# Attention and expert mix on one core: a prologue in another order, and two expert slots per pass of a shared PSUM bank

## What is computed

```python
xn = _layernorm(x)
# attention, 16 heads of width 8; q = k = v
p = einsum('bsd,ed->bse', xn, Wv) + bv
attn = softmax(einsum('bhqd,bhkd->bhqk', p, p) / sqrt(8))
s = einsum('bsd,ed->bse', einsum('bhqk,bhkd->bhqd', attn, p), Wo) + bo
# 8 experts, the best 2 of each token, weighted
z = layernorm(xn, ln_g, ln_b)
w = top-2 of softmax(z @ rW + rb), divided by their sum
mixed = sum_e w_e * (gelu(z @ W1[e] + b1[e]) @ W2[e] + b2[e])
out = x + s * silu(xn + mixed)
```

## Time and profile before

| | |
|---|---|
| three executions | 628.3, 629.17, 630.58 us; median 629.17 us |
| the profiled execution | 632.46 us, of which the span from the first to the last instruction is 630.7 us |
| PE | 571.2 us busy (91% of the span) |
| ACT | 543.2 us busy (86%), of which 488.9 us in the 512 exponentials |
| DVE, POOL | 240.1 us (38%), 230.1 us (36%) |
| mean granted PE clock | 0.936 |
| step 0 to step 255 by the exponentials | 52.73 to 620.54 us |

### The profile page before, as it was taken

The page is one execution under the profiler, slowest core; times in us unless marked ns, Lnnn a source line. Parts: engine busy times, 40 slices in busy tenths (PEclk is TensorE's granted clock), DMA queues, the critical chain, the costliest instruction groups (busy, mean ns, idle before and its releaser), DMA issues.

```text
span 630.7 us, 11527 instructions
## 1 busy us (share of the span) xinstructions
PE 571.2 (91%) x3990; PEld 232.3 (37%) x3990; DVE 240.1 (38%) x695; ACT 543.2 (86%) x591; POOL 230.1 (36%) x252
## 2 busy tenths in 40 slices
PE   3778884799999999799999999999988999999996
PEld 2553320223344344333444344434334343433221
DVE  5553863573333333113222232223232852223381
ACT  4576663699999999979999999999999999999994
POOL 2364047827777774254211121112203334341000
PEclk9977776799999999869999999999995999999999
DMA  6137697746466655227363445453233654442220
GB/s 164 45 101 219 231 304 276 184 132 149 110 162 133 162 96 116 70 67 160 68 153 99 127 112 132 103 135 108 70 117 108 173 167 139 130 116 83 65 66 19
DMA packets 100989, 81.54 MB, mean 129 GB/s; under 512 B 54219, under 2 KB 92638, under 8 KB 100318
## 3 DMA queue, kind: packets, MB, share of 16 engines
q1 hardware_dynamic: 94270, 71.26, 43.2%
q0 software_dynamic: 6656, 9.48, 4.8%
HBM read 58.07 MB, written 28.39 MB: 137 GB/s over the span
## 4 chain that ended last, share of the span: by engine, by line
PE 74%; ACT 9%; DVE 7%; issue 5%; DMA 4%; SPq 1%; ACTq 0%; DVEq 0%
PE bank_v L1330 35%; PE pair L1276 16%; PE bank_f L1370 8%; PE bank_f L1379 8%; ACT exps L776 7%; DMA p_dram<-w_ring 3%; PE bank_f L1347 2%; PE pair L1236 1%; ACT pre L752 1%; PE bank_f L1343 1%; PE pair L1227 1%; DMA x_tok<-in_L_attn_x 1%; DVE o_turned L1082 1%; PE bank_f L1354 1%; DVE v_tok L863 1%
## 5 line engine op out<-in xcount | busy, mean ns | idle before, releaser
L776 ACT ACTIVATE exps<-pair 128x1024 f32<-128x1024 f32 x512 | 488.9, 1049 | 54.6 <-PE pair L1276 36.3
L1330 PE MATMUL bank_v<-exps,v_tok 128*32 128x512 f32 x2048 | 285.0, 630 | 3.1 <-ACT exps L776 1.6
L687 POOL DMA_INDIRECT o_dram<-o_ring,slot_place x80 | 77.4, 968 | 238.3 <-DVE o_ring L1133 238.0
L1276 PE MATMUL pair<-q_ring,k_ring 26*128 26x512 f32 x1024 | 152.9, 513 | 2.7 <-ACT exps L776 2.1
L1276 PEld LDWEIGHTS pair<-q_ring,k_ring 26*128 26x128 f32 x1024 | 60.7, 188 | 93.4 <-ACT exps L776 54.8
L672 POOL DMA_INDIRECT z_dram<-pre,dest_i x64 | 64.3, 1004 | 52.2 <-DVE place_i L1037 33.3
L1379 PEld LDWEIGHTS bank_f<-w_ring,pre 128*128 128x128 f32 x320 | 46.2, 208 | 72.2 <-issue 43.3
L1124 DVE TENSOR_TENSOR pre<-bank_f,w_ring 128x256 f32<-128x256 f32 x80 | 33.9, 423 | 102.1 <-PE bank_f L1370 102.1
L1379 PE MATMUL bank_f<-w_ring,pre 128*128 128x128 f32 x320 | 62.5, 322 | 9.7 <-ACT pre L752 5.3
L1133 DVE TENSOR_TENSOR o_ring<-bank_f,w_ring 128x128 f32<-128x128 f32 x80 | 23.2, 290 | 124.3 <-PE bank_f L1379 121.1
L679 POOL DMA_INDIRECT place_dram<-token_place,place_i x64 | 61.3, 958 | 19.5 <-issue 19.5
(11 more groups left out here) (154 smaller groups left out, 287.1 us busy)
## 6 DMA issues: line engine op xcount, KB each, us to landing
w_ring<-w_dram SPq DMA_DIRECT2D x80, 192.0 KB
w_ring<-w_dram SPq DMA_DIRECT2D x80, 129.0 KB
q_ring<-p_dram SPq DMA_DIRECT2D x56, 104.0 KB
k_ring<-p_dram SPq DMA_DIRECT2D x56, 96.0 KB
z_dram<-s_tok SPq DMA_DIRECT2D x4, 1280.0 KB, 13.1
z_ring<-z_dram SPq DMA_DIRECT2D x80, 64.0 KB
rows_in_sb<-o_dram SPq DMA_DIRECT2D x16, 256.0 KB, 2.9
p_dram<-z_ring SPq DMA_DIRECT2D x8, 256.0 KB, 2.9
```

The costliest lines, as they stand in the source:

```text
L687: pool.indirect_dma_start(o_dram[:, :], bass.IndirectOffsetOnAxis(slot_place[:, h, 4 * k + i:4 * k + i + 1].bitcast(U32), 0), o_ring[:, q ...
L776: nc.scalar.activation(exps[:, g % ES, 2 * half:2 * half + 2, :], pair[(2 * g + half) % 3][:, :, :], ACT.Exp, scale=SCALE).then_inc(exp_do ...
L1276: ins = nc.tensor.matmul(pair[h % 3][:, j % 2, :], k_ring[32 * j:32 * j + KROWS, n % 2, kt * P:(kt + 1) * P], q_ring[32 * j:32 * j + KROWS ...
L1330: ins = nc.tensor.matmul(bank_v[32 * j:32 * j + 32, :], v_tok[:, (n // HG) * KT + kt, first:first + 32], exps[:, g % ES, j, :], start=(kt ...
```

## The change

**The bank.** One use now holds two slots of a quad (`PAIRS` = 2 uses per quad instead of four): `up` writes all 512 columns of `bank_f` with four matmuls, and DVE reads 128x512 at once; `down` writes 256 columns with four matmuls. So 80 uses stand where 160 stood, and `MOE_STEP` is 2.52. The bursts at the two Gelu stretches (now steps 90 and 185) hold all eight `down` slots of two quads in four uses.

**The early steps.** `count` moves from step 7 to 8, the biases from 4..6 and 8..12 to 9..16, the `norm` uses from 13..18 to 23, 25, ... 33, the ranking of the first half one step later, `zero_z(1)` from step 12 to 8, scaling of the first expert layer from 13..16 to 18..21.

**The prologue.** The second chunk of `x` is loaded earlier; the four warming matmuls at the head of the branch that is taken go; on DVE the third chunk of `norm1` stands ahead of `keep_p(0)` instead of behind it, and `norm2` moves out of the loop over blocks, behind the branch. On SP the high part of blocks 0 and 1 is stored three times, so that units 0 and 1 (eight heads) are each loaded with 8 DMAs, after blocks 3 and 4; `w1_stage`, `rb_bc` and `bo_bc` are loaded behind all blocks; the copy in DRAM covers three batches instead of four and is issued for step 14.

```diff
+EARLY_PARTS = 4
...
-WARM = (4, 4)
+WARM = 4
...
-RANK_AT = ((2, 3, 3, 4, 4, 5), (17, 18, 19, 20, 22, 23))
-COUNT_AT = (7, 24)
-ASSIGN_AT = ((7, 8, 8, 9, 10), (25, 26, 27, 28, 30))
+RANK_AT = ((3, 4, 4, 5, 5, 6), (17, 18, 19, 20, 22, 23))
+COUNT_AT = (8, 24)
+ASSIGN_AT = ((8, 9, 9, 10, 11), (25, 26, 27, 28, 30))
 SCALE_Z_AT = ((5, 6, 7, 8), (18, 20, 22, 23))
-EXP_AT = (10, 21)
+EXP_AT = (11, 21)
 WEIGH_AT = ((12, 13, 14), (31, 32, 33))
-BIAS_AT = 4
+BIAS_AT = 9
+COPY_HI_AT = 14
 BIAS_COLS = 2
-NORM_AT = 12
-ZERO_AT = 12
-SCALE_W1_AT = (13, 14, 15, 16)
-SCATTER_AT = (11, 31)
-MOE_AT = 37
-MOE_STEP = 1.19
+NORM_AT = 23
+ZERO_AT = 8
+SCALE_W1_AT = (18, 19, 20, 21)
+SCATTER_AT = (12, 31)
+MOE_AT = 38
+MOE_STEP = 2.52
 LOAD_LAG = 5
 PLACE_AT = (54, 77)
-BURST = 6
+PAIRS = 2
...
-        for i in range(4):
+
+        for i in range(PAIRS):
             t = max(t, place((kind, q, i), t) + 1 - MOE_STEP) + MOE_STEP
...
-        downs = [("down", first + i // 4, i % 4) for i in range(8)]
-        uses[g] = downs[:BURST]
+        uses[g] = [("down", first + i // PAIRS, i % PAIRS) for i in range(2 * PAIRS)]
         at.update({what: g for what in uses[g]})
-        t = g + 3
-        for what in downs[BURST:]:
-            t = max(t, place(what, t) + 1 - MOE_STEP) + MOE_STEP
-        return g, t
+        return g, g + 3
...
-        place(("norm", g), NORM_AT + g - EARLY)
+        place(("norm", g), NORM_AT + 2 * (g - EARLY))
...
+        def stored(g):
+
+            return 16 * (EARLY_PARTS + g // 2 * PARTS)
...
             load_x(1)
+            load_x(2)
...
+            def load_unit(n):
+                if n >= 2:
+                    sp.wait_ge(pv_done, (n - 1) * US)
+                if n == HG:
+                    sp.wait_ge(hi_copied, 32)
+                    for i in range(2):
+                        sp.wait_ge(m_kept[1 + i], (NB - EARLY) // 2 * 16)
+                tokens = slice((n // HG) * S, (n // HG + 1) * S)
+                for j in range(4):
+                    head = (n % HG) * 4 + j
+                    sp.dma_start(k_ring[32 * j:32 * j + PROWS, n % 2, :].bitcast(F32), p_dram[head, 0:PROWS, tokens]
+                                 ).then_inc(kq_in[n % 2], 16)
+                    sp.dma_start(q_ring[32 * j:32 * j + KROWS, n % 2, :].bitcast(F32), p_dram[head, HI_ROW:HEAD_ROWS, tokens]
...
             for g in range(NB):
                 tokens = slice(g * BLK, (g + 1) * BLK)
                 sp.wait_ge(parts_ready, g + 1)
-                for part in range(PARTS):
-                    row = (HI_ROW, LO_ROW)[part]
-                    sp.dma_start(p_dram[:, row:row + DK, tokens], (p_hi, p_lo)[part][:, g % 2, :]).then_inc(parts_stored[g % 2], 16)
-                if g == EARLY:
+                hi_rows = (0, HI_ROW, LO_ROW + DK) if g < EARLY else (HI_ROW,)
+                for row in hi_rows:
+                    sp.dma_start(p_dram[:, row:row + DK, tokens], p_hi[:, g % 2, :]).then_inc(parts_stored[g % 2], 16)
+                sp.dma_start(p_dram[:, LO_ROW:LO_ROW + DK, tokens], p_lo[:, g % 2, :]).then_inc(parts_stored[g % 2], 16)
+                if g == 2:
                     for e in range(EARLY):
                         sp.wait_ge(n2_copied, e + 1)
                         sp.dma_start(p_dram[:, M_ROW, e * BLK:(e + 1) * BLK], m_blk[:, e, :]).then_inc(m_kept[0], 16)
-                    for i in range(2):
-                        sp.wait_ge(parts_stored[i], 16 * PARTS)
+                elif g == 3:
+                    for e in range(EARLY):
+                        sp.wait_ge(parts_stored[e], stored(e))
                     sp.wait_ge(m_kept[0], 16 * EARLY)
                     sp.wait_ge(m_zeroed, 32)
                     sp.wait_ge(ring_cleared, 1)
-                    for j in range(4):
-                        load_head(0, 0, j, 0, kq_in[0])
-                        load_stabiliser(0, j, kq_in[0])
-                if g == 3:
-                    sp.dma_start(w1_stage, W1.rearrange("e h f -> h e f")).then_inc(w1_staged, 16)
-                    sp.dma_start(rb_bc[:, :], rb.rearrange("(a d) -> a d", a=1).broadcast_to([P, E])).then_inc(bias_in, 16)
-                    sp.dma_start(bo_bc[:, :], bo.rearrange("(a d) -> a d", a=1).broadcast_to([P, D])).then_inc(bias_in, 16)
+                    load_unit(0)
+                elif g == 4:
+                    load_unit(1)
+            sp.dma_start(rb_bc[:, :], rb.rearrange("(a d) -> a d", a=1).broadcast_to([P, E])).then_inc(bias_in, 16)
+            sp.dma_start(w1_stage, W1.rearrange("e h f -> h e f")).then_inc(w1_staged, 16)
+            sp.dma_start(bo_bc[:, :], bo.rearrange("(a d) -> a d", a=1).broadcast_to([P, D])).then_inc(bias_in, 16)
+            zero_z(0)
             for i in range(2):
-                sp.wait_ge(parts_stored[i], NB // 2 * 16 * PARTS)
+                sp.wait_ge(parts_stored[i], stored(NB - 2 + i))
...
-            zero_z(0)
-            load_unit(1)
             for g in range(STEPS + 1):
                 n, k = divmod(g, US)
                 if k == VLAG and 1 <= n < NU - 1:
                     load_unit(n + 1)
-                if g == 2:
+                if g == COPY_HI_AT:
                     for row in (0, LO_ROW + DK):
-                        sp.dma_start(p_dram[:, row:row + DK, :], p_dram[:, HI_ROW:HI_ROW + DK, :]).then_inc(hi_copied, 16)
+                        sp.dma_start(p_dram[:, row:row + DK, EARLY * BLK:], p_dram[:, HI_ROW:HI_ROW + DK, EARLY * BLK:]).then_inc(hi_copied, 16)
...
-                    pool.wait_ge(parts_stored[g % 2], g // 2 * 16 * PARTS)
+                    pool.wait_ge(parts_stored[g % 2], stored(g - 2))
...
-            keep_p(0)
             norm1(2, *NORMS[2])
-            for g in range(1, NB):
+            for g in range(NB):
                 keep_p(g)
                 if g == 1:
                     keep_n2(0)
                     keep_n2(1)
                 elif g == 3:
                     choose_m_row()
-                elif g == 4:
-                    norm2()
...
+                    ins = nc.vector.tensor_tensor(
+                        pre[:, k, 2 * i * HF:2 * (i + 1) * HF].rearrange("p (s c t) -> p s c t", s=2, c=FC),
+                        bank_f[:, :].rearrange("p (s c t) -> p s c t", s=2, c=FC),
+                        w1_ring[:, q % 2, 2 * i:2 * i + 2, HF:W1W].unsqueeze(3).broadcast_to([P, 2, FC, P]), ALU.add)
                 elif what == "down":
                     q, i = arg
                     if i == 0:
                         dve.wait_ge(w2_in[q % 2], (q // 2 + 1) * 16 * 4)
                         if q >= 2:
                             dve.wait_ge(o_stored[q % 2], q // 2 * 64)
-                    ins = nc.vector.tensor_tensor(o_ring[:, q % 2, i, :], bank_f[:, 0:D], w2_ring[:, q % 2, i, FC * D:W2W], ALU.add)
+                    ins = nc.vector.tensor_tensor(o_ring[:, q % 2, 2 * i:2 * i + 2, :], bank_f[:, 0:2 * D].rearrange("p (s d) -> p s d", s=2),
+                                                  w2_ring[:, q % 2, 2 * i:2 * i + 2, FC * D:W2W], ALU.add)
                 ins.then_inc(bank_f_read, 1)
...
+            norm2()
             keep_router_bias()
...
-                keep_warm(WARM[1])
                 prologue()
...
-                    for c in range(FC):
-                        ins = nc.tensor.matmul(bank_f[:, c * P:(c + 1) * P], w1_ring[:, q % 2, i, c * P:(c + 1) * P],
-                                               zT[:, q % 2, i * P:(i + 1) * P], start=True, stop=True)
+                    for a, c in itertools.product(range(2), range(FC)):
+                        slot = 2 * i + a
+                        ins = nc.tensor.matmul(bank_f[:, (a * FC + c) * P:(a * FC + c + 1) * P], w1_ring[:, q % 2, slot, c * P:(c + 1) * P],
+                                               zT[:, q % 2, slot * P:(slot + 1) * P], start=True, stop=True)
```

More of the change, by code:

```diff
@@ L2 @@
+import itertools
 from contextlib import ExitStack
@@ L169, in timetable @@
             order[what] = len(order)
-    load = [at["down", (h + 1) * QUADS - 1, 3] + LOAD_LAG for h in range(HALVES)]
+    load = [at["down", (h + 1) * QUADS - 1, PAIRS - 1] + LOAD_LAG for h in range(HALVES)]
     return uses, at, order, gelu, load
@@ L410, in _ @@
             sp.dma_start(rw_sb[:, :], rW).then_inc(small_in, 16)
-            for c in range(2, len(X_CHUNKS)):
+            for c in range(3, len(X_CHUNKS)):
                 load_x(c)
@@ L479, in _ @@
             with sp.If(m2_bits > M2_LIMIT_BITS):
-                sp.wait_ge(kq_in[0], 16 * KQ_FIRST)
+                for i in range(2):
+                    sp.wait_ge(kq_in[i], 16 * KQ_LOADS)
                 with sp.Fori(0, NU // 2) as w:
@@ L698, in _ @@
                     for i in range(4):
-                        if g == AT["down", q, i]:
+                        if g == AT["down", q, i // 2]:
                             store_o(q, i)
```

62 lines of the change are left out of this document (21 added, 41 removed).

## The result

The changed kernel took **645.76 us** (median of four, 642.29 to 648.24), the kernel before 629.04 (628.3 to 630.58): a ratio of 1.025, 95% interval 1.020 to 1.030. It is **slower by 2.5%**, where 605.5 us and a gain of 24 were forecast. The ratios of the experiments are to the kernel before on the same chip, 629.0 to 630.8 us; where two experiments are compared by their times and ran on different chips, up to 1.8 us of the difference can be the chips'.

A forecast was written before the change was run, and what follows sets the result against it. It took the steady expert part as PE-bound (2.01 us per step), stretches without expert uses as paced by ACT (1.81). Early steps -25.2 and experts +1.5 gave -23.7: profiled 632.46 to 608.8, median 605.5 us, range 596 to 619.

The forecast's parts named there:

- step 0 starts: End of the prologue: first step at 42 us instead of 52.73, between 40 and 45, with unit 0's load last.
- steps 9 to 17: Eight steps with a bias each and no norm: 21 us instead of 30.15, bounds 16.5 and 26.
- steps 17 to 24: No waits for norm or expert-weight stores: 14 us instead of 20.65, step 24 at 102.5 instead of 127.68.
- The norm uses of steps 23 to 33: Moved norm uses, one bf16 matmul: claimed to fit into PE's lead over ACT and cost nothing.
- the lead: What a free step (no use) gives PE over ACT: 1.81 - 1.62 = 0.19 us, no more however many follow.
- Rival D: Expert part: PE's short waits in free steps pull the clock down, slower than before, 644 us; chance 0.03.
- Step 9: Starts at 67.5 us instead of 76.88; DVE waits for bo_bc until 57 to 57.5, ranking then takes 9.
- the two norm waits: Norm uses waiting for an earlier norm's store, 12.68 and 6.90 us before the change; claimed to go.
- The doubling, +1.5 us: Expert part: doubled use 1.08 us, its step 2.51; experts in all +1.5 us, bounds -5 and +8.
- Rival A: Expert part: PE's saved time counts, giving 15 + 2 us instead of costing 1.5; 587 us, chance 0.10.
- rival C: Expert part: the doubled use is dearer, 0.2 us on each of 80; 621 us, chance 0.09.

The follow-up runs named there:

- e1: Changed kernel with keep_w2 and clear_places issued right behind the copy in DRAM, where SP is idle: 633.44 us, ratio 1.004.
- e2: Changed kernel with load_z(0) and load_z(1) issued ahead of keep_w2, clear_places and the load of unit 3: 633.54 us, ratio 1.004.
- e3: e1 with the first w1 loads and the first z loads also issued four steps earlier: 623.98 us, ratio 0.988.
- e9: Changed kernel with only the norm uses put back early, at steps 17, 18, 20, 22, 23 and 25: 637.52 us, ratio 1.010.
- e6: e3 with rb_bc and bo_bc loaded behind the last chunk of x: 617.45 us, ratio 0.980.
- e5: e3 with all 16 bias columns in one use at step 7, ahead of count 0: 610.54 us, ratio 0.972.
- e8: e3 with PE's wait ahead of count 0 filled by 30 repeated score matmuls in step 8: 624.59 us, ratio 0.993.
- e13: e3 with all 16 bias columns in one use at step 12, behind PE's wait ahead of count 0: 613.21 us, ratio 0.973.
- e11: e12's kernel with the eight loads of unit 1 issued behind the stores of block 7 instead of block 4: 610.10 us, ratio 0.968.
- e4: e3 with one expert slot per pass of the bank and bursts of six, as before the change: 621.83 us, ratio 0.984.
- e12: e3 with the edits of e5 and e6 together, a repeat run: 606.98 us, ratio 0.964.
- e10: e12's kernel with one expert slot per pass of the bank, as before the change: 604.02 us, ratio 0.958.

## Why the prediction was wrong, and where it was right

The forecast of the profiled execution was 608.8; it took 642.3. Step by step, in us:

| term | forecast | measured | difference |
| --- | --- | --- | --- |
| step 0 starts | 42 | 45.60 | +3.6 |
| steps 0 to 9 | 25.5 | 26.93 | +1.4 |
| steps 9 to 17 | 21 | 28.32 | +7.3 |
| steps 17 to 24 | 14 | 14.19 | +0.2 |
| steps 24 to 38 | 25.7, as before | 26.18 | +0.5 |
| a wait at step 38 | none | 21.2 (23.47 less 2.3) | +21.2 |
| experts behind it, against before | +1.5 | +0.7 (465.4 less 464.7) | -0.8 |

Together 33.4 of 33.5. The median of the changed kernel is 3.5 us above this profiled execution, where the forecast took it as 3.3 below, which makes the 40.3 us between the forecast and the measured median.

- **The step that failed: "The norm uses of steps 23 to 33 (one bf16 matmul) fit into the lead and cost nothing."** For PE it is right: steps 25 to 34 take 1.81 to 1.89. But each norm has a store on SP that waits for it, and what is queued behind these stores on SP I did not follow past step 24. The edit of `NORM_AT` moved the stores from steps 14 to 19 to steps 24 to 34. The last one that SP had to wait for is now that of step 30, issued at 129.70, with 24 us of list behind it; in place of nothing it cost a wait of 21.2 us at step 38. e1, e2, e3 and e9 show it. None of my rivals held this. Rival D, slower than before, had the price (644) for another mechanism: the expert part it spoke of ran at 1.00, free steps among doubled uses and all, but for the stretches around the stall and the two Gelu stretches. The rule of the Trainium skill beside it ("TensorE: Matmul & The Clock Gate", section "A second HAM failure mode: psum-queue depth-cycling") did not act there.
- **Steps 9 to 17, "the other steps cost 2.1 to 2.3 us"**: mis-sized. At 2.4 GHz that would do (e6 has 1.97 for such a step); measured are 3.54 at 1.2 GHz. I had looked at the clock for the expert part only. e5, e8 and e13 show that the bias uses in each step hold it low; what would have warned me is the granted clock of before in the same stretch, 0.76 over 62 to 75 us, 0.97 over 75 to 85 and 0.57 over 85 to 93 (row below, columns as in the earlier trace rows). The sentence of rival D that the clock "went down to 1.2 GHz only behind long gaps" was wrong of that trace too: it went down at 85.84, and in the ten us ahead PE's longest wait is 1.55 us.

```profile
85.00:93.00 8.00, 8.00 (x43) 2.57 (x43) 3.37 (x12) 4.93 (x6) 6.17 (x7) 0.57 0.94 312
```

- **Step 0, "They land by about 41.5 to 42 (2.9 for the nearest transfer)"**: the loads were issued from 36.93 to 40.2, somewhat later than forecast (38.8), and landed some 4.5 us later, at 44.77. A row of before of stores from SBUF was no measure for loads of 24 and 26 rows out of DRAM. What sets the 4.5 is open; unit 1 is not it (e11).
- **Step 9**: `bo_bc` as the last wait was right, its time 5 us off (issued at 55.7, landed 6.8 later). From L881 to the end of the ranking it took 8.6 us (9 forecast). e6 confirms the wait: 6.5 us are gone with it.
- **Step 17 to 24**, and the end of the two norm waits of the earlier trace rows: right. No norm's store is in the chain of the changed kernel.
- **The doubling, +1.5 us**: sign and mechanism right. A doubled use takes 1.09, its step 2.51 to 2.53, 2.3 behind a free step, free steps 1.81 to 1.82. The size was taken too small: side by side it is 2.2 (e3, e4) and 3.0 us (e12, e10). Rival A (the saved PE time counts) and rival C (0.2 more per use) fall. My sign for them was a bad one: the steps from 39 on average 2.15 us, "over 2.1", but they did so in the kernel before as well.

With its SP queue, its biases and `bo_bc` mended the change gives about what was forecast of it (607 against 605.5), and 604 without the doubled bank. That is luck: the last two edits, 17 us of it, are not in the change that I forecast, and the terms still miss and cancel. In e12 step 0 is 4.4 us later than forecast, and steps 9 to 24 take 29.3 us instead of 35.
